# Gated recurrence, routed feed-forward, context experts and 64 routed experts on one core: the first dense layer and the context experts become one written-out block of 16 units, with its first two weight sets split during the recurrence

## What is computed

```python
# layer 0: a gated recurrence over the 512 tokens of each row
z = sigmoid(x_t @ W_z + h @ U_z + v_z);  r = sigmoid(x_t @ W_r + h @ U_r + v_r)
h = (1 - z) * h + z * tanh(x_t @ W + (r * h) @ U + v)          # v: cond_1024 @ C + b
# layer 0: a feed-forward block for the better half of the tokens of each row
weights   = h_all @ w_r + b_r
selected  = weights > (256th largest of the row)
x = x + where(selected, gelu(h_all @ W1 + b1) @ W2 + b2, h_all)
# layer 1: context experts, 2 of 4 per row by a gate, and one shared expert
y = gelu_tanh(x @ sw1 + sb1) @ sw2 + sb2
y = y + sum over the row's 2 experts e: w_be * mask_e * (gelu_tanh(x @ ew1[e] + eb1[e]) @ ew2[e] + eb2[e])
# layer 1: routed experts, 8 of 64 per token, at most 160 tokens each, and a shared one (swiglu)
x = x + shared(y) + sum over the token's 8 experts: gate * expert(y)
```

## Time and profile before

| | us |
|---|---|
| median of 3 runs | 2236.54 |
| lowest and highest run | 2231.12, 2237.56 |
| the profiled execution's own time | 2228.02 |
| its span, first to last instruction | 2226.2 |
| PE busy | 2136.7 (96%) |
| DVE, ACT, POOL busy | 1537.2, 860.0, 458.7 |
| recurrence, to its last PE instruction | 0 to 1046 |
| first dense layer | 1048 to 1157 |
| context experts | 1162 to 1427 |
| routing and shared expert | 1429 to 1566 |
| 64 routed experts | 1566 to 2226 |

### The profile page before, as it was taken

The page is one execution under the profiler, slowest core; times in us unless marked ns, Lnnn a source line. Parts: engine busy times, 40 slices in busy tenths (PEclk is TensorE's granted clock), DMA queues, the critical chain, the costliest instruction groups (busy, mean ns, idle before and its releaser), DMA issues. The chain is left out here.

```text
span 2226.2 us, 80746 instructions
## 1 busy us (share of the span) xinstructions
PE 2136.7 (96%) x31909; PEld 1953.9 (88%) x31909; DVE 1537.2 (69%) x8706; ACT 860.0 (39%) x3348; POOL 458.7 (21%) x610
## 2 busy tenths in 40 slices
PE   9999999999999999998999999999999999999997
PEld 8898888889889888887778888866899999999997
DVE  6777777777777777777644455485577777777775
ACT  3343333333333333334555676633222222222221
POOL 0000000000000000000310000154455555555553
PEclk9999999999999999999999999999999999999998
DMA  3000000000000000001002123210788888888882
GB/s 122 4 4 4 4 4 4 4 4 4 4 4 4 4 4 4 4 4 41 0 0 84 58 94 112 104 57 26 263 283 268 276 277 268 283 265 284 264 280 61
DMA packets 55533, 213.39 MB, mean 96 GB/s; under 512 B 11578, under 2 KB 40960, under 8 KB 46976
## 3 DMA queue, kind: packets, MB, share of 16 engines
q1 hardware_dynamic: 36276, 184.41, 22.7%
q0 software_dynamic: 17408, 23.61, 5.7%
q10 hardware_dynamic: 1484, 0.40, 0.1%
HBM read 192.82 MB, written 15.57 MB: 94 GB/s over the span
## 5 line engine op out<-in xcount | busy, mean ns | idle before, releaser
L1479 PE MATMUL bank<-xe,ring 128*128 128x160 f32 x3072 | 440.8, 300 | 0.5 <-ACT xe L1498 0.5
L1479 PEld LDWEIGHTS bank<-xe,ring 128*128 128x128 f32 x3072 | 425.0, 191 | 0.9 <-issue 0.9
L1522 DVE STREAM_TRANSPOSE turned<-ye 32x64 f32<-32x64 f32 x1240 | 291.4, 235 | 16.2
L526 PE MATMUL bank<-keep_part,Us 128*128 128x4 f16 x6132 | 286.0, 168 | 0.3 <-DVE keep_part L449 0.3
L526 PEld LDWEIGHTS bank<-keep_part,Us 128*128 128x128 f16 x6132 | 242.7, 105 | 12.4 <-DVE keep_part L449 0.4
L526 PE MATMUL bank<-h_part,Us 128*128 128x4 f16 x6144 | 242.6, 167 | 0.9 <-DVE h_part L469 0.9
L1434 POOL DMA_INDIRECT out_rows<-res,to_row x128 | 192.3, 1503 | 244.6 <-DVE res L1541 210.5
L337 POOL TENSOR_TENSOR hist<-ring,unscale 128x128 f32<-128x128 f32 x32 | 16.4, 513 | 1029.2 <-DVE ring L465 1029.2
L1507 ACT ACTIVATE gate_f<-bank 128x160 f32<-128x160 f32 x384 | 116.8, 304 | 288.5 <-PE bank L1479 283.4
L314 ACT ACTIVATE r_h<-bank 128x8 f32<-128x8 f32 x512 | 93.2, 182 | 346.4 <-PE bank L526 346.4
L526 PE MATMUL bank<-step_high,Us 128*128 128x4 f16 x4096 | 193.1, 169 | 34.5 <-DVE step_high L453 3.4
(11 more groups left out here) (235 smaller groups left out, 3773.5 us busy)
## 6 DMA issues: line engine op xcount, KB each, us to landing
ring<-in_ew SPq DMA_DIRECT2D x64, 2304.0 KB
raw<-in_L_cond_ew SPq DMA_DIRECT2D x16, 1024.0 KB, 6.2
ctx_rows<-rows SPq DMA_DIRECT2D x2, 1280.0 KB, 6.7
dense_w<-in_L_ffn_W SPq DMA_DIRECT2D x2, 1024.0 KB, 6.3
raw<-in_L_cond_sw SPq DMA_DIRECT2D x2, 1024.0 KB, 6.2
out_rows<-orow SPq DMA_DIRECT2D x4, 512.0 KB, 2.9
out_rows<-res,to_row POOLq DMA_INDIRECT x128
xT<-in_xT SPq DMA_DIRECT2D x2, 864.0 KB, 8.5
```

Source lines behind the costliest of these rows:

```text
L526: last = nc.tensor.matmul(pre[g][q][:, jj, m, :], Us[:, g, p, k, m * P:(m + 1) * P], x[part][:, k * B:(k + 1) * B], start=False, stop=Fals ...
L1479: last = nc.tensor.matmul(bank[f % UPS][:, s_ * CAP:(s_ + 1) * CAP], w1[u][:, k, s_ * FFN + f * P:s_ * FFN + (f + 1) * P], xe[e % 2][:, k] ...
L1522: last = nc.vector.transpose(y[:, :, q, :], ye[e % 2][q * SQ:(q + 1) * SQ, :, j * SQ:(j + 1) * SQ])
```

## The change

- One block fewer: `layer0_ffn` and `layer1_context` become `dense`, with no hardware loops: 4 units of the first dense layer and 12 of the context experts are written out on every engine.
- The split of the first dense weights and of the shared expert's moves into the recurrence. From span 2 on, at steps 10, 16, 22, 28 and 34 of a span, ACT copies one piece of 512 columns after its own work (16 in all), and in each of the four steps after it DVE subtracts a quarter, 128 columns (64 in all). The router weights are spread in span 1. SP loads both weight sets at the recurrence's start.
- In a dense unit the comparisons come one tile later, the count after the last tile. The scores, the mask and the selected values lie in `raw`. The split of x for the context is done row by row within the dense units (ACT after tile 4, DVE after tile 5), by DVE where POOL did three of the four rows. ACT's tables are loaded once per use ahead of the loops.
- In routing, row 0's mask turns come after down group 0 instead of ahead of both, the `shift` product after group 1.
- Idle matmuls (ones times zeros, 128x128 by 128x512 bf16, nobody reads them): 7 at the end of `dense`, 8 ahead of the last `turn_base` and 5 behind it. POOL zeroes their input at the start.

```diff
 MEET = ((0, 0), (1, 0), (0, 1))
+def keep_busy(nc, to, ones_bf, rows, n):
+    for _ in range(n):
+        nc.tensor.matmul(to[:], ones_bf[:], rows, start=True, stop=True)
+
+
 def program(nc, A, out):
...
-        with ExitStack() as dense:
-
-            raw = dense.enter_context(nc.sbuf_tensor("raw", [P, FF], F32))
-            parts = [[dense.enter_context(nc.sbuf_tensor(f"weights{q}_part{p}", [P, FF], F32R)) for p in range(2)] for q in range(2)]
-            layer0_ffn(nc, sem, bank, xT, hist, ident, ones_bf, (wr, br, b1, b2, dense_w[:, 0:FF]), s_ffn,
-                       lambda eng: load_gate(eng, raw),
-                       s_shared, raw, parts)
-            layer1_context(nc, sem, A, bank, xT, hist, ident, ones, condT, (gw, gb, tw, tb, eb1, eb2),
-                           raw, parts, s_gate, load_router)
+        wr_rep = cut(FF, KD, P)
+        idle_rows = sb("idle_rows", [P, S], BF16)
+
+        with ExitStack() as weights:
+
+            raw = weights.enter_context(nc.sbuf_tensor("raw", [P, FF], F32))
+            parts = [[weights.enter_context(nc.sbuf_tensor(f"weights{q}_part{p}", [P, FF], F32R)) for p in range(2)] for q in range(2)]
+            gru(nc, sem, A, bank, xT, hist, ident, ones, ones_bf, condT, slot_row, s_x, s_const,
+                lambda eng: (load_ffn(eng), load_gate(eng, raw)),
+                (dense_w[:, 0:FF], s_ffn, 96), (raw, s_shared, 64), parts, wr, wr_rep, idle_rows)
+            dense(nc, sem, A, bank, xT, hist, ident, ones, ones_bf, condT, wr_rep, (br, b1, b2),
+                  (gw, gb, tw, tb, eb1, eb2), raw, parts, s_gate, load_router, idle_rows)
...
         def place(j):
             return j // SPAN, j % SPAN
+
+        CHUNK = 512
+        CHUNKS = ffn_raw[0].shape[1] // CHUNK
+        NEXT = 2 * CHUNKS
+        FIRST_AT, EVERY, LOWS = 10, 6, 4
+        PER_SPAN = (SPAN - FIRST_AT) // EVERY
+        LOW = CHUNK // LOWS
+
+        def next_piece(i, a=0, z=CHUNK):
+            source, part = ((ffn_raw, next_parts[1]), (shared_raw, next_parts[0]))[i // CHUNKS]
+            at = i % CHUNKS * CHUNK
+            return source[0][:, at + a:at + z], part[0][:, at + a:at + z], part[1][:, at + a:at + z]
+
+        def turn_of(span, jj):
+            i, n = (span - 2) * PER_SPAN + (jj - FIRST_AT) // EVERY, (jj - FIRST_AT) % EVERY
+            return (i, n) if span >= 2 and jj >= FIRST_AT and i < NEXT else (None, 0)
+
...
                         seed(span + 1, turn // TERMS, turn % TERMS)
                     if span + 2 < SPANS and jj == HIGH_AT:
                         high_inputs(span + 2)
+                    i, n = turn_of(span, jj)
+                    if i is not None and n == 0:
+                        if i % CHUNKS == 0:
+                            act.wait_ge(s_ffn if i == 0 else s_shared, ffn_raw[2] if i == 0 else shared_raw[2])
+                        whole, high, low = next_piece(i)
+                        nc.scalar.activation(high, whole, ACT.Copy).then_inc(s_nhi, 1)
             @block.gpsimd
             def _(pool):
...
+                nc.gpsimd.memset(idle_rows[:], 0.0)
                 nc.gpsimd.memset(unscale[:], 2.0 ** -STATE_EXP).then_inc(s_unscale, 1)
                 pool.wait_ge(s_unscale, 1)
                 for g in range(S // SEG):
...
                     if span + 2 < SPANS and jj in LOW_AT:
                         dve.wait_ge(s_xhi, span + 3)
                         low_inputs(span + 2, (LOW_AT.index(jj),))
+                    if span == 1 and 0 <= jj - SPAN // 2 < KD:
+                        k = jj - SPAN // 2
+                        dve.wait_ge(s_ffn, ffn_raw[2])
+                        nc.vector.tensor_copy(wr_rep[:, k], wr[:, k:k + 1].to_broadcast([P, P])).then_inc(s_rep, 1)
+                    i, n = turn_of(span, jj)
+                    if i is not None and 1 <= n <= LOWS:
+                        dve.wait_ge(s_nhi, i + 1)
+                        whole, high, low = next_piece(i, (n - 1) * LOW, n * LOW)
+                        nc.vector.tensor_tensor(low, whole, high.bitcast(F32), ALU.subtract).then_inc(s_nlo, 1)
             @block.tensor
             def _(pe):
...
+                for b in range(B):
+                    for k in range(KD):
+                        last = nc.tensor.matmul(bank[0][:], wr_rep[:, k], hist[:, k, b], start=(k == 0), stop=(k == KD - 1))
+                    last.then_inc(s_sp, 1)
+                    pe.wait_ge(s_stlo, b + 1)
+                    for f in range(KH):
+                        up_tile(b, f, FFN_UP, w1[1], state)
+                        if f == 1:
+                            pe.wait_ge(s_s, b + 1)
+                            for j in range(S // P):
+                                last = nc.tensor.transpose(bank[1][:, j * P:(j + 1) * P], ws[:, j * P:(j + 1) * P], ident[:])
+                            last.then_inc(s_tp, 1)
+                        if f == KH - 1:
+                            pe.wait_ge(s_ge, b + 1)
+                            for j in range(S // P):
+                                last = nc.tensor.matmul(bank[2][:], ones_bf[:], ge[:, j], start=(j == 0), stop=(j == S // P - 1))
+                            last.then_inc(s_cnt, 1)
+                    down(b, w2[1])
...
+                def context_unit(m, b, q):
+                    for f in range(KH):
+                        up_tile(m, f, CONTEXT_UP, w1[q], [v[:, :, b] for v in xs])
+                    down(m, w2[q])
                 def shared(b):
                     pe.wait_ge(s_xlo, b + 1)
-                    unit(b, b, 0)
-
-                def chosen(b, k):
-                    pe.wait_ge(s_wlo, expert(b, k) * PIECES + PIECES)
-                    unit(expert(b, k) + B, b, place(k))
-
+                    context_unit(SHARED + b, b, 0)
+
+                pe.wait_ge(s_m, B)
                 shared(0)
...
-                with pe.Fori(1, B) as b:
+                for b in range(1, B):
                     shared(b)
...
+                def hidden(m, f, up, bias, func):
+                    act.wait_ge(s_fp, m * KH + (f + 1))
+                    if f >= 2:
+                        act.wait_ge(s_flo, m * KH + (f - 1))
+                    nc.scalar.activation(hid[0][:, f], up[f % len(up)][:], func, bias=bias[:, f:f + 1])
+                    nc.scalar.activation(full[:, f % 2], up[f % len(up)][:], func, bias=bias[:, f:f + 1]).then_inc(s_f, 1)
+
+                high_states(0)
+                nc.scalar.activation(silu_c[:], condT[:], ACT.Silu).then_inc(s_silu, 1)
...
-                def unit(m, b, u, out_of, split_next=None):
+                    act.wait_ge(s_sp, b + 1)
+                    nc.scalar.activation(ws[:], bank[0][:], ACT.Identity, bias=br[:, 0:1]).then_inc(s_s, 1)
                     for f in range(KH):
-                        act.wait_ge(s_fp, m * KH + (f + 1))
-                        if f >= 2 or not isinstance(m, int) or m:
-                            act.wait_ge(s_flo, m * KH + (f - 1))
-                        nc.scalar.activation(hid[0][:, f], up[f % len(up)][:], ACT.Gelu_apprx_tanh, bias=b1[:, u, f:f + 1])
-                        nc.scalar.activation(full[:, f % 2], up[f % len(up)][:], ACT.Gelu_apprx_tanh,
-                                             bias=b1[:, u, f:f + 1]).then_inc(s_f, 1)
-                    if split_next:
-                        split_next()
+                        hidden(b, f, FFN_UP, fb1, ACT.Gelu)
...
                     nc.vector.tensor_tensor(hid[1][:, f], full[:, f % 2], hid[0][:, f].bitcast(F32), ALU.subtract).then_inc(s_flo, 1)
+
+                def low_x(b):
+                    dve.wait_ge(s_xhi, b + 1)
+                    nc.vector.tensor_tensor(xs[1][:, :, b], xT[:, :, b, 0:S], xs[0][:, :, b].bitcast(F32), ALU.subtract).then_inc(s_xlo, 1)
+
+                low_states(0)
+                for b in range(B):
+                    for f in range(KH):
+                        low_tile(b, f)
+                        if b and f == 5:
+                            low_x(b - 1)
+                        if f == 2:
+                            dve.wait_ge(s_tp, b + 1)
+                            nc.vector.tensor_copy(wcol[:], bank[1][:].rearrange("p (j c) -> p j c", c=P)[:, :, 0]).then_inc(s_t, 1)
+                        if f == 3:
+                            dve.wait_ge(s_t, b + 1)
+                            dve.wait_ge(s_s, b + 1)
+                            for j in range(S // P):
+                                last = nc.vector.tensor_scalar(ge[:, j], ws[:], wcol[:, j:j + 1], None, ALU.is_le)
+                            last.then_inc(s_ge, 1)
+                    dve.wait_ge(s_cnt, b + 1)
...
@@ -1180,13 +1104,6 @@
                             pe.wait_ge(s_ot, 1)
                             nc.tensor.transpose(bank[6][:, 0:P], order[:, 1, 0:P], ident[:])
                             nc.tensor.transpose(bank[7][0:CAP - P, 0:P], order[:, 1, P:CAP], ident[:]).then_inc(s_ot, 1)
-                    if b == 0:
-
```

(28 more changed lines are left out.)

373 lines of the change are left out of this document (124 added, 249 removed).

## The result

| | before | after |
|---|---|---|
| median of the timed runs | 2237.0 us (2231.1 to 2237.6, 4 runs) | 2203.7 us (2203.0 to 2206.3, 4 runs) |
| ratio | | 0.9859, 95% interval 0.9841 to 0.9878 |
| profiled execution, own time and span | 2228.0, 2226.2 us | 2206.3, 2204.3 us |

What follows compares the result with a forecast made beforehand. PE, at work 96% of the span, bounds the kernel through idle stretches, low clock and the recurrence. Terms 4.5 + 7.2 + 1.7 + 7.5 + 2.4 = 23.3 us; 2236.5 - 23.3 gives 2213 us, range 2204 to 2222.

Steps and rivals of the forecast that it cites:

- A: Recurrence to dense layer: wait on the count gone, some slow clock gone, scores start earlier; 4.5 us saved, between 3.4 and 7.2.
- B: Dense layer to context: the 4.99 us idle stretch and the slow 48 products after it vanish; 7.2 us saved.
- F: Recurrence: the inserted copies and subtraction quarters fit its gaps, just in time; cost 0.
- C: Context to routing: 7 idle matmuls keep the clock up, the border's idle 2.31 us stays; 1.7 us saved, 0 if not.
- D: Routing's mask turns: down group 0 fills the wait, turns and group 1 at full clock; 7.5 us saved.
- E: Routing to experts: idle matmuls hold the clock for the first 24 up products; 2.4 us saved, 0 if not.
- G: Loops written out in the dense units: no gain or cost counted, 0.
- the rivals: Lost clock 0.11, new dense-block stall (2216 us) 0.06, larger gain 0.06, half-paid recurrence (2230) 0.04, fully paid (2248) 0.03.
- the lost clock: Idle matmuls do not hold the clock, C and E lost, 4.1 us: 2217 us; chance 0.11.
- the larger gain: Clock rises at once in A, or the recurrence's longer steps fall otherwise; 4 us more, 2209 us; chance 0.06.

Runs made afterwards that it cites:

- runs 8 and 9: Second chip, both unaltered: the kernel before (2229.2 us, span 2228.3) and the changed kernel (2201.3 us, ratio 0.9878, span 2199.4).
- run 4: Changed kernel with the count product back behind tile 5 and the comparisons back behind tile 2 in the dense units: 2204.7 us.
- run 10: Changed kernel with five idle matmuls of 512 columns behind PE's last product of the recurrence: 2201.3 us, the unaltered change also 2201.3.
- run 5: Changed kernel with an unused 16-byte tile allocated ahead of the parts of x and the hidden units: 2211.7 us, against 2201.3 unaltered.
- its mirror: Kernel before with its 16-byte tile of score columns allocated behind the dense stage's other tiles: 2223.7 against 2228.7 us, ratio 0.998.
- run 2: Changed kernel without its three groups of idle matmuls: 2209.8 us, 5.1 us slower than the unaltered change on the same chip.
- run 3: Changed kernel with row 0's mask turns back ahead of the first down group, shift product behind group 0: 2213.0 us, 8.3 us slower than unaltered.
- run 6: Changed kernel with DVE's subtraction of each 512 weight columns in one piece instead of four quarters: 2206.1 us, 4.8 us more than unaltered.
- runs 1 and 9: The changed kernel again, unaltered: 2204.6 us (ratio 0.987) on the first chip, 2201.3 us (ratio 0.9878) on the second.

## Why the prediction was right, and where it was not

The forecast was faster, 2213 us, 2204 to 2222. The median of the first comparison, 2203.7, lies 0.3 us below that range. The sum against the profiled execution, 2204.7, was met within 2 us (2206.3). That closeness is partly luck: in the first pair of traces below, 2.6 us that the sum did not have on the side of the gain (A, B and routing) stand against 4.0 us on the other side (start, recurrence and a late gate). **The step that failed** is the last one: adding the 8.5 us by which before's median stood above its profiled execution. That excess was no constant. The changed kernel never showed it (three sets of runs, medians 2201.3 to 2204.6), and on the second chip neither did before (2228.7). On chips on which before spreads to 2237, the change takes away the spread too; where in before it sits is open, since both traces of it are of executions near 2228.

The terms, as measured in two pairs of traces (the first comparison; and runs 8 and 9, on one chip), in us saved:

| from, to | forecast | first pair | second pair |
|---|---|---|---|
| start and recurrence | F = 0 | -1.2 | -0.4 |
| last product of the recurrence to unit 2 | A = 4.5 | 5.3 | 7.9 |
| unit 2 to the context's gate | B = 7.2 | 8.8 | 9.2 |
| context steady to routing | 0 | 0 | 0 |
| start of routing to the first expert's downs | C + D + E = 11.6 | 11.8 | 12.2 |
| first expert's downs to the second's | 0 | -2.8 | 0 |
| sum | 23.3 | 21.9 | 28.9 |

- **A** was right in what it counted and wrong in why. The 3.4 us wait is gone. The prediction laid it to DVE, which "still subtracted weights"; the rows under run 4 show DVE idle after that, and its comparisons stretched beside POOL's split. Both left the place with the change, so the term came out all the same, by luck of the edit. It was undersized, because before's first unit varies (32.0 and 33.6 us) and the pace of the products was not in it. The slow scores stayed, and idle matmuls in front did not help them (run 10).
- **B**: 7.2 us at the seam, as forecast (4.99 idle, 2.19 in the first 48 products). Most of the other 1.6 us, 0.5 in each of units 2 to 4, is the pace of 226.7 instead of 233.3 ns. The prediction had no such term; run 5 and its mirror show where it comes from. The seam itself is read from the two traces; no run puts the border back.
- **C** came out at 1.6 us for a forecast 1.7, but for a reason that run 2 does not bear out: without the idle matmuls the clock stayed up as well, after the same 2.31 us. What keeps it up in the changed kernel is open.
- **D** was right in size and mechanism: 7.5 us between the traces, 7.8 in the undoing (run 3).
- **E** was right up to the first expert's down products: 2.35 us, and 1.9 us in the undoing. The rule in the Trainium skill ("TensorE: Matmul & The Clock Gate", Part 4: PE-mode transpose), that a transpose does not count as PE work in the same way, did not cost the term: with eight turns, 1.09 us, between two groups of idle matmuls the clock stayed at 1.00 (stretch 1545 to 1549 above). In the first pair 2.8 us were given back at once in a wait that the prediction did not look at, though before's trace had its smaller form (0.94 us). On the second chip E stays whole.
- **F**: right but for a fraction of a microsecond. The median step is 1.993 us in both, also at the steps with a quarter, and run 6 shows the price of the same work in larger pieces; "just in time" was the right reading of the earlier trace rows. The occasional longer steps fall elsewhere and are a few more: from the first r to the last pass 1022.7 to 1023.0 us in the three traces with the old recurrence and 1023.1 to 1024.1 in the ten with quarters. The other 0.8 us of the first pair lie ahead of the first step.
- **G**: the written-out loops brought PE nothing by themselves: in before, the fourth unit, which was always written out, runs at the pace of the looped ones. That the loops show no stall is no disagreement with the rule that the prediction names: no trace shows that their targets lay outside the fetched pages.

Of the signs that the prediction named, most came: no idle bracket on the count, none between the dense layer and the context, 10.64 us for the 64 products, 0.19 us on the mask turns, 3.50 us for the first expert products. The first score product starts 1.74 us behind the recurrence instead of 2.48, but at 1048.85 and not 1047.8, since the recurrence ends later. One sign of being wrong came too: PE's idle time from 1430 to 1560 is 3.8 us in the first trace, above the 3 us named, 2.09 of it the wait for the first expert's gate; in runs 1 and 9 it is 2.5 and 1.7 us.

Of the rivals, none came. At the places it named the lost clock did not happen in the changed kernel; the larger gain did in part, through A and the pace, as its line said only loosely.

## What to carry over

Undo a change part by part before believing its terms: here one term had the right size for an unproven reason (C), and the theory of the count's place, read from two traces, fell with one run. When an engine is late, look at the length of what it runs last, not only at what stood in its list before: the comparisons had grown from 1.67 to 4.38 us (A). When timed runs lie above the profiled execution, do not carry the excess over to the changed kernel; keep it as a width of the range. And compare the start-to-start distance of equal products before and after: a layout side effect of 3% is worth as much as a wait, and no idle bracket shows it.

## What was not expected of the hardware

- The start address of the moving tiles (x, states and hidden units) set the pace of 512-column products of two-part f32 data: 233.3 ns behind a 16-byte tile, 226.7 ns without it, with the weights left in place. Over 16 units this made 10.3 us.
- VectorE's comparisons of 128x512 took 0.83 and 1.48 us each while GpSimd split weights (0.48 us each while it was idle), in all three traces with the old dense stage. No run varies this alone.
- An idle stretch of 2.31 us was followed by 12.3 us for 64 products in three traces of before kinds, and by 10.64 us in run 2. The length of the idle stretch alone does not tell whether the clock falls.
- Five idle matmuls (2.29 us) right behind the recurrence did not speed up the four score products behind them: 3.65 and 3.53 us, and 3.37 to 3.78 us in all other traces.
- Late gates of the first expert, up to 4.3 us, in all five traces of changed kernels from the first comparison and the first chip, in none of the six from the second. Of the kernel before, the first trace has a smaller one (a wait of 0.94 us), the two on the second chip none. The first expert's down products then started 1.3 to 5.3 us further ahead of the second's than the usual 10.0 us. The cause is open.
